# Gating loop: factors and weights kept in PSUM, and VectorE's work on the chunk behind cut into four parts

## The reference, cut to what matters

```
h = (x_flat @ W_gat).reshape(M, HEADS, NUM_EXPERTS)          # 4 heads, 4 experts: 16 numbers a node
a_src = (h * att_src).sum(-1);  a_dst = (h * att_dst).sum(-1)
e = leaky_relu(a_src[src] + a_dst[dst], 0.2)                 # one score per edge and head
e_max = segment_max(e, dst)
ee = exp(e - e_max[dst])
denom = segment_sum(ee, dst)
agg = segment_sum(h[src] * (ee / (denom[dst] + 1e-16))[:, :, None], dst)
scores = layernorm(agg + b_gat, ...).mean over heads         # then top 2 of 4 experts, softmax, expert MLPs
```

## Time and profile before

| | |
|---|---|
| median of 3 runs | 2664.83 us (2663.48 to 2666.10) |
| profiled execution | 2667.64 us, of which its span 2665.8 us |
| busy, of the span | DVE 1932.1 us (72%), POOL 1769.0 us (66%), PE 1203.0 us (45%), ACT 535.9 us (20%) |
| chain that ended last | POOL 60%, issue 20%, DVE 10%, PE 6% |
| 1900 to 2000 us, inside the loop | PE 87.72, DVE 86.75, POOL 77.72, ACT 26.32 us of 100 |
| granted TensorE clock there | 0.93 of full speed |

### The profile page before, as it was taken

How to read it: one execution, slowest core, us unless ns; L and a number is a source line. 1 busy time by engine, 2 the same in 40 slices (tenths; PEclk the granted TensorE clock), 3 DMA queues, 4 the chain that set the end, 5 groups by cost and what they waited for, 6 DMA issues and landing times.

```text
span 2665.8 us, 34021 instructions
## 1 busy us (share of the span) xinstructions
PE 1203.0 (45%) x12499; PEld 1007.2 (38%) x12499; DVE 1932.1 (72%) x3127; ACT 535.9 (20%) x640; POOL 1769.0 (66%) x1690
## 2 busy tenths in 40 slices
PE   3874000000001001010214399589889898898286
PEld 2532000000000000000113255379889898887266
DVE  7588596988687878787888501168888888888356
ACT  1010002222222223131201011222222222222121
POOL 0001877777777777774677677777777777777470
PEclk9976555555555555555555555579989899899658
DMA  9500213233333333231222706112121222221101
GB/s 299 193 1 23 72 38 106 86 118 101 98 105 93 107 94 115 86 116 50 70 75 51 97 6 186 23 25 25 24 40 25 39 25 25 40 25 24 30 9 33
DMA packets 145715, 186.75 MB, mean 70 GB/s; under 512 B 84845, under 2 KB 103983, under 8 KB 139167
## 3 DMA queue, kind: packets, MB, share of 16 engines
q1 hardware_dynamic: 91494, 121.12, 14.6%
q0 software_dynamic: 54080, 63.61, 13.9%
HBM read 97.32 MB, written 87.32 MB: 69 GB/s over the span
## 4 chain that ended last, share of the span: by engine, by line
POOL 60%; issue 20%; DVE 10%; PE 6%; DMA 1%; ACT 1%; SPq 1%; POOLq 0%; DVEq 0%
POOL arena L729 56%; DVE arena L1359 7%; PE psum L933 2%; POOL d_adseed L816 2%; POOL d_qseed L753 1%; PE psum L1095 1%; SPq L569 1%; DVE arena L1362 1%; PE psum L1126 1%; PE psum L1011 1%; DVE psum L1761 1%; PE psum L1023 1%; ACT arena L1201 0%; DVE arena L1782 0%; DVE arena L1764 0%
## 5 line engine op out<-in xcount | busy, mean ns | idle before, releaser
L1359 DVE TENSOR_TENSOR arena<-arena 128x512 f32<-128x512 f32 (+18 forms) x1347 | 802.8, 635 | 160.7 <-ACT arena L1165 53.1
L729 POOL DMA_INDIRECT arena<-d_h,arena x668 | 696.4, 1042 | 203.7 <-issue 203.4
L729 POOL DMA_INDIRECT arena<-in_kv,arena x640 | 648.1, 1013 | 199.0 <-issue 194.5
L1050 PE MATMUL psum<-arena 128*128 128x128 bf16 x10080 | 613.6, 224 | 92.6 <-DVEq L1969 90.6
L1050 PEld LDWEIGHTS psum<-arena 128*128 128x128 bf16 x10080 | 600.1, 100 | 97.2 <-DVE arena L1362 94.9
L849 PE MATMUL psum<-arena 128*128 128x128 f32 (+3 forms) x402 | 90.0, 391 | 1100.2 <-DVEq L1435 1004.1
L849 PEld LDWEIGHTS psum<-arena 128*128 128x128 f32 (+3 forms) x402 | 68.7, 202 | 1122.7 <-DVEq L1435 1019.3
L1362 DVE TENSOR_SCALAR arena<-arena 128x512 bf16<-128x512 f16 (+9 forms) x1067 | 339.6, 376 | 67.7 <-ACT arena L1265 24.6
L1359 DVE TENSOR_TENSOR arena<-psum,arena 128x512 f32<-128x512 f32 (+2 forms) x179 | 167.2, 942 | 207.8 <-PE psum L1011 202.6
L729 POOL DMA_INDIRECT arena<-d_adst,arena x40 | 54.4, 1360 | 257.5 <-DVEq L1606 245.6
L1761 DVE TENSOR_TENSOR_SCAN psum<-psum,arena 128x1024 f32<-128x1024 f32 x40 | 91.9, 2298 | 137.0 <-ACT arena L1188 136.0
(11 more groups left out here) (184 smaller groups left out, 1385.5 us busy)
## 6 DMA issues: line engine op xcount, KB each, us to landing
d_gs<-arena SPq DMA_DIRECT2D x32, 768.0 KB
d_as<-arena SPq DMA_DIRECT2D x20, 1152.0 KB, 4.5
d_qseed<-arena SPq DMA_DIRECT2D x5, 4096.0 KB, 29.8
arena<-d_qseed SPq DMA_DIRECT2D x20, 1024.0 KB, 6.0
arena<-d_h,arena POOLq DMA_INDIRECT x668
arena<-in_kv,arena POOLq DMA_INDIRECT x640
d_adseed<-arena SPq DMA_DIRECT2D x1, 4096.0 KB, 29.4
arena<-d_adseed SPq DMA_DIRECT2D x17, 128.0 KB
```

The lines of the kernel that those rows point to most:

```text
L729: return pool.indirect_dma_start(out, None, table, bass.IndirectOffsetOnAxis(index[:, t:t + 1], 0))
L1050: last = nc.tensor.matmul(ps[2 + turn_of(b, m)][:, k * PICK_W:(k + 1) * PICK_W], pick_hot[turn_of(b, m)][:, t, k * P:(k + 1) * P], h_split ...
L1359: return V.tensor_tensor(o, a_, b_, op)
```

## The change

Two spaces in PSUM, free during the loop, take the carry factors (`g_keep`, 1300 columns) and the weights (`g_weight`, 260 columns) of the chunks inside the loop; the first chunk, ahead of it, keeps them in SBUF. ScalarE writes the weights twice, once to PSUM for the product and once to SBUF as the last 260 columns of the scan's input. `maximum` is split into `edge_scores` and `maximum`, `weighted_sums` into `messages` and `weighted_sums`, and the four go behind takes 0, 1, 2 and 3. In ScalarE's program `lay` moves ahead of the keys of batch 3 and `rows` behind the keys of batch 6.

```diff
+        g_keep = psum[:, 4 * 512:4 * 512 + G_F * G_COLS]
+        g_weight = psum[:, 7 * 512:7 * 512 + G_HEADS * G_COLS]
...
             def weigh(it, b, back):
                 act.wait_ge(g_max_set, it * 2 + (b - 2 * back * b + 1))
+                keep = g_keep if back else g_corr_f
+                if back:
+                    nc.scalar.activation(g_weight, g_em, ACT.Exp)
                 nc.scalar.activation(g_msg[:, G_HF * G_COLS:], g_em, ACT.Exp).then_inc(g_exp_done, 1)
-                nc.scalar.activation(g_corr_f[:, G_HF * G_COLS:], g_dm, ACT.Exp).then_inc(g_exp_done, 1)
+                nc.scalar.activation(keep[:, G_HF * G_COLS:], g_dm, ACT.Exp).then_inc(g_exp_done, 1)
...
-                nc.scalar.copy(g_corr_f[:, 0:G_HF * G_COLS].rearrange(...), bc(g_corr_f[:, G_HF * G_COLS:]...))
+                nc.scalar.copy(keep[:, 0:G_HF * G_COLS].rearrange(...), bc(keep[:, G_HF * G_COLS:]...))
...
                         all_keys(it, b, 2)
+                        lay(it, 1 - b, 1)
                         all_keys(it, b, 3)
-                        lay(it, 1 - b, 1)
                         all_keys(it, b, 4)
                         weigh(it, 1 - b, 1)
                         all_keys(it, b, 5)
+                        all_keys(it, b, 6)
                         rows(it, 1 - b, 1)
-                        all_keys(it, b, 6)
...
-            def maximum(it, b, back, first=False):
+            def edge_scores(it, b, back):
                 c1 = it * 2 + (b - 2 * back * b + 1)
                 dve.wait_ge(g_laid, c1)
...
                 link(it, b, back, V.scalar_tensor_tensor(x_, x_, 0.2, x_, ALU.mult, ALU.max))
+
+            def maximum(it, b, back, first=False):
                 if not first:
                     dve.wait_ge(g_rows_set, it * 2 + (b - 2 * back * b))
...
-            def weighted_sums(it, b, back):
+            def messages(it, b, back):
                 dve.wait_ge(g_weighed, it * 2 + (b - 2 * back * b + 1))
-                w = g_msg[:, G_HF * G_COLS:].rearrange("p (h j) -> p h j", j=G_COLS)[:, :, 1:]
+                w = (g_weight if back else g_msg[:, G_HF * G_COLS:]).rearrange("p (h j) -> p h j", j=G_COLS)[:, :, 1:]
...
                 dve.sem_inc(g_used, 1)
-                link(it, b, back, V.tensor_tensor_scan(g_sum, g_corr_f, g_msg, 0.0, ALU.mult, ALU.add))
+
+            def weighted_sums(it, b, back):
+                link(it, b, back, V.tensor_tensor_scan(g_sum, g_keep if back else g_corr_f, g_msg, 0.0, ALU.mult, ALU.add))
                 dve.sem_inc(g_summed, 1)
...
                         for m in range(BATCHES - 2):
                             one_hot(it, b, m + 2)
                             take_picked(it, b, m)
-                            if m == 1:
-                                maximum(it, 1 - b, 1)
-                            if m == 2:
-                                weighted_sums(it, 1 - b, 1)
+                            if m < 4:
+                                (edge_scores, maximum, messages, weighted_sums)[m](it, 1 - b, 1)
```

More of the change, by code:

```diff
@@ L1250, in weigh @@
                 nc.scalar.copy(g_msg.rearrange("p (f j) -> p f j", j=G_COLS)[:, :, 0], before_sum if back else zeros[:, 0:G_F])
-                nc.scalar.copy(g_corr_f[:, 0:G_HF * G_COLS].rearrange("p (h k j) -> p h k j", h=G_HEADS, j=G_COLS),
-                               bc(g_corr_f[:, G_HF * G_COLS:].rearrange("p (h j) -> p h j", j=G_COLS)[:, :, None, :],
+                nc.scalar.copy(keep[:, 0:G_HF * G_COLS].rearrange("p (h k j) -> p h k j", h=G_HEADS, j=G_COLS),
+                               bc(keep[:, G_HF * G_COLS:].rearrange("p (h j) -> p h j", j=G_COLS)[:, :, None, :],
                                   [P, G_HEADS, G_EXP, G_COLS])).then_inc(g_weighed, 1)
@@ L1979, in _ @@
             flags(0, 0, 0)
+            edge_scores(0, 0, 0)
             maximum(0, 0, 0, True)
+            messages(0, 0, 0)
             weighted_sums(0, 0, 0)
@@ L2016, in _ @@
                         flags(it, 1 - b, 1)
+                        edge_scores(it, 1 - b, 1)
                         maximum(it, 1 - b, 1)
+                        messages(it, 1 - b, 1)
                         weighted_sums(it, 1 - b, 1)
```

## The result

| | before | after |
|---|---|---|
| median | 2665.34 us (2663.48 to 2666.10) | 2713.91 us (2711.29 to 2716.59, 4 runs) |
| span of the profiled execution | 2665.8 us | 2714.5 us |

The change makes the kernel slower: ratio 1.0186, 95% interval 1.0173 to 1.0198. The prediction said 2732 us (2686 to 2772).

What follows compares the result with a forecast made beforehand. Two nearly equal chains were taken as the bound: GpSimd's gathers (49.1 us) and scan, rows, indices, keys (47.9). Fourteen passes +83.4, last pass -2.6, end wait -13.5 make +67.3, giving 2732 us (2686 to 2772).

Steps and rivals of the forecast that it cites:

- Two chains nearly equal: Gating loop before: GpSimd's gathers take 49.1 us a chunk; scan, rows, indices and keys take 47.9 a pass.
- freeing GpSimd shows only at the end: Loop's end: VectorE's 16.08 us wait for the last gathers falls to some 3.3, with `lay`'s copies: -13.5 us.
- index leg: From the end of ScalarE's row copies to `pick_keys`, while the indices load: 5.7 us, between 5.4 and 6.1.
- Operands in PSUM free GpSimd: Two long gathers a chunk fall to about 0.95 us, saving 3.2; GpSimd's pace goes from 49.1 to 45.9.
- The product's -0.42: VectorE's weighted product falls from 2.29 to 1.87 us with a PSUM operand, bounds -0.6 and +0.1.
- The scan one batch later: VectorE's long scan stands behind one more batch (4.55 us) and ends 27.6 us into the pass, not 23.40.
- Keys to flags: From `pick_keys` to the next flags: 14.25 us plus 2.2 for batch 6 at a slower TensorE clock.
- The last pass: Chunk 16's pass, which makes no next keys, falls from 43.4 us to 41: -2.6.
- A: Rival: TensorE's clock holds, so the 2.2 us a pass drops out: 2701 us, chance 0.14.
- B: Rival: GpSimd's release decides and the wait for indices does not grow: faster, 2629 us, chance 0.09.
- C: Rival: GpSimd is not freed, its pace stays 49.1 us; time still 2732, counted in the forecast's 0.73.
- D: Rival: no change, with index leg and clock at their good ends: about 2665 us, chance 0.04.

Runs made afterwards that it cites:

- e1: Kernel before with only factors and weights moved to PSUM, every engine's order kept: 2651.63 us, ratio 0.9948.
- e5: Kernel before, with SyncE loading the next indices behind `g_used` and writing the rows out afterwards: 2664.99 us, ratio 1.0002.
- e10: Kernel before with factors and weights in PSUM and SyncE loading the indices ahead of the rows' write-out: 2651.05 us, ratio 0.9952.
- e2: Changed kernel's four parts and new ScalarE order, but factors and weights kept in SBUF: 2725.75 us, ratio 1.0219.
- e3: Changed kernel with the long scan put back directly behind the product, behind take 2: 2650.99 us, ratio 0.9943.
- e4: Changed kernel, with SyncE loading the next indices behind `g_used` alone and waiting for the rows only before the write-out: 2657.13 us, ratio 0.9970.
- e7: Changed kernel with TensorE doing batch 6 ahead of the next chunk's first two spreads: 2693.12 us, ratio 1.0106.
- e9: Changed kernel with 27 tiny clears on GpSimd between the 36 gathers of a chunk: 2718.50 us, ratio 1.0204.
- e6: Changed kernel with 96 more matmuls on TensorE in each pass, ahead of the next chunk's first spread: 2720.28 us, ratio 1.0203.

## Why the prediction was right, and where its sizes were off

**Two chains nearly equal, and freeing GpSimd shows only at the end: right.** e1 has it alone: passes -0.14 us, the median -14.5 us to the before beside it (predicted at the end: -13.5). In after that term measured -13.8. But the second chain is not the index leg alone: with early indices the passes stay 47.85 (e5) and 47.73 (e10), so another chain, of VectorE's own work and its waits for TensorE's results, is as long. What sets it stays open.

**Operands in PSUM free GpSimd: right.** Two chunks' first gathers are 52.87 apart, less a wait of 6.79: 46.08 us a chunk, 45.9 predicted. The scan kept 2.87. The product's -0.42 failed: 2.29 in SBUF and in PSUM, so the attention loop's 1.87 was the wrong row to price it by. The same pairs of numbers, with one of two operands moved, speak on the Trainium skill, "VectorE: DVE Perf Modes", the section on the TRN2 errata: its 62 cycles more for a PSUM source are in neither the product nor the scan. And what the Trainium skill infers in "SBUF — State Buffer" (who interferes with whom), that two SBUF inputs leave descriptor making alone, does not hold for these gathers: 2.67 and 3.51 us in e2, 1.37 at most between 2020 and 2125 us in after, with one operand moved. The gathers read their indices from SBUF as well (`arena<-d_h,arena`), and the same section of the Trainium skill does have two SBUF inputs contend with a GpSimd instruction that reads SBUF, which the prediction left out.

**The scan one batch later: right** (27.6; 27.78), with some luck: the 0.42 that the product did not give were nearly made up, as it started 0.33 us earlier in the pass (17.97 for 18.30 in the mean). Right, too, is the step on which all hangs, that `rows` (4.10; 4.10), write-out and index loads follow it while `pick_keys` comes no later. e3 and e4 show both: the scan back, or the loads off the scan, and the loss is gone.

**The index leg was mis-sized:** 5.7, with bounds 5.4 and 6.1; 4.43 measured, outside the bounds. At 1.27 us in 14 passes it is -17.8 us, most of the 18 by which 2732 is too long. The 5.4 was no reading of the leg: in that row the keys wait for VectorE itself, and in e5, where the indices come early, the keys start 9.50 to 9.56 us behind the scan's end, as they did there (9.52). The longer legs I had taken from passes in which GpSimd issued gathers all the while; in after GpSimd's last gather had ended 4.4 to 7.4 us before the indices came. e2, where it ended 1.0 to 4.3 us before in all passes but one, has a mean leg of about 5.25, which fits.

What the DMA queues moved from the end of the row copies to the keys differs as well (queue, packets, MB, share; q1 has SyncE's transfers, q0 GpSimd's gathers, q8 instructions). First the pass of before that follows rows 3, with a leg of 5.99, then after's pass above, with 4.57:

```profile
q1 hardware_dynamic: 720, 1.02, 46.1%
q0 software_dynamic: 150, 0.05, 22.4%
q8 instruction: 1, 0.02, 1.4%
...
q1 hardware_dynamic: 705, 1.01, 63.5%
```

In before each of the seven legs over 5.5 has such an instruction transfer begin 0.6 to 1.0 us behind the copies. e7 had legs of 6.2 to 6.7 with the last gather 4.3 to 5.4 us before: each of these seven has an instruction transfer inside, and none of its six legs of 4.4 to 4.9 has one. Here a leg of 6.46 (keys at 2058.27) and one of 4.62 (keys at 2108.42):

```profile
q0 software_dynamic: 64, 0.02, 4.5%
q8 instruction: 1, 0.02, 0.9%
...
q0 software_dynamic: 64, 0.02, 9.7%
```

So a long leg goes with gathers or an instruction transfer beside the index loads. No run moved either by itself (e9 did not move GpSimd), so that they lengthen the leg is likely and not shown.

**Keys to flags:** 14.25 + 2.2 = 16.45; 16.00 measured, -6 us in all. TensorE's wait (9; 8), the half clock and batch 6 (7.7; 7.3 in the mean) came as said. The surcharge of 2.2 is what e6's six passes give (16.00 against 13.80); the 14.25 under it was 0.45 too long.

**The last pass:** -2.6 predicted, -0.6 measured; its closing steps still wait for batch 6 (3.88 us for TensorE).

With the measured terms: 67.3 - 20.9 (passes) + 2.0 (last pass) - 0.3 (end) = 48.1, against 48.7; the loop's later start is 0.2 of the rest.

**Rivals.** A: the clock did not hold (0.50). B: VectorE reached `pick_keys` 4.1 us before the indices, so GpSimd's release could not decide. C: GpSimd was freed. D: the index leg came out shorter than its good end, and the passes still took 52.31.

## What to carry to other kernels

Price a moved instruction by what its completion releases on other queues, here a copy, a write-out and the loads behind it in SyncE's order. Work that fills one engine's hole can hold up a transfer that three engines wait for; take the transfer off that instruction, or leave the instruction where it is. Where an engine is freed of time that another chain hides, expect only what stands uncovered at the loop's end. And a leg should be priced from a place in which it is what the next step waits for, and in which the neighbours do what they will do after the change.

## What was not expected of the hardware

- The 128x1024 product takes 2.29 us with its strided operand in SBUF whether the other lies in SBUF or in PSUM.
- With the same transfers, the leg from the row copies to the indices is 4.2 to 4.8 us in after's loop and 5.2 to 6.5 in e1, where gathers run beside it, in seven of the 13 passes an instruction transfer too.
- A clear of 128x2 on GpSimd (0.11 to 0.25 us) between two gathers does not spread them: they stay 1.25 us apart.
- In every pass of e2 and of before, the gather that runs beside a product or scan from SBUF ends 0.74 to 0.76 us after that instruction does, once 0.87 (in e2's pass above 2.67 and 3.51 us in place of 0.95).
